# A graph network on one core: three layernorm chunks placed behind the listed rows, shorter update stages, and units of 58 blocks

## What is computed

```python
src, dst = edge_index                      # 25000 edges, dst sorted
denom = jnp.maximum(segment_sum(ones, dst, 50000), 1.0)
conv = lambda x, W, b: segment_sum(concatenate([x[src], edge_attr], axis=1) @ W + b, dst, 50000) / denom[:, None]
outputs = [conv(x, W0, b0)]                # x is 50000 x 128
for W, b in ((W1, b1), (W2, b2), (W3, b3)):
    outputs.append(conv(concatenate(outputs, axis=1), W, b))
result = layernorm(x + outputs[-1])        # over 128 columns, eps 1e-5
```

## Time and profile before

| | us |
|---|---|
| median of three runs | 1026.16 (1024.44 to 1027.6) |
| the profiled execution, its own time | 1026.18 |
| its span, first to last instruction | 1024.2 |
| POOL busy | 719.3 (70%) |
| DVE busy | 698.9 (68%) |
| ACT busy | 497.8 (49%) |
| PE busy | 462.8 (45%) |

### The profile page before, as it was taken

The page is one execution under the profiler, slowest core; times in us unless marked ns, Lnnn a source line. Parts: engine busy times, 40 slices in busy tenths (PEclk is TensorE's granted clock), DMA queues, the critical chain, the costliest instruction groups (busy, mean ns, idle before and its releaser), DMA issues.

```text
span 1024.2 us, 13421 instructions
## 1 busy us (share of the span) xinstructions
PE 462.8 (45%) x2853; PEld 343.8 (34%) x2876; DVE 698.9 (68%) x2449; ACT 497.8 (49%) x1322; POOL 719.3 (70%) x660
## 2 busy tenths in 40 slices
PE   3343663776765899988726300550046661000000
PEld 2342553554443566654415200440035451000000
DVE  6995888788766787667477586659479963798000
ACT  6552765666563667566532155624474640366200
POOL 6674777677771777777767387748777774777775
PEclk9565665656665899999966555675557766555555
DMA  6799569499999476755567389957999982653110
GB/s 181 235 289 271 148 151 295 118 330 318 318 311 339 167 242 230 235 200 190 197 199 248 121 205 298 344 184 191 300 301 349 316 275 56 198 165 134 52 51 32
DMA packets 224614, 224.90 MB, mean 220 GB/s; under 512 B 19218, under 2 KB 206475, under 8 KB 224495
## 3 DMA queue, kind: packets, MB, share of 16 engines
q1 hardware_dynamic: 193551, 153.22, 48.3%
q0 software_dynamic: 26624, 44.81, 16.3%
q10 hardware_dynamic: 4320, 25.56, 6.2%
HBM read 117.11 MB, written 132.74 MB: 244 GB/s over the span
## 4 chain that ended last, share of the span: by engine, by line
DVE 24%; POOL 20%; DMA 16%; issue 12%; PE 11%; ACT 6%; SPq 6%; DVEq 2%; ACTq 1%; POOLq 0%
POOL G L674 6%; POOL out_rows L713 5%; SPq L491 4%; POOL part_rows L687 4%; POOL x_and_z_of_nodes L657 4%; DVE area L1040 3%; DMA G<-part_rows,s0r 3%; DMA x_and_z_of_nodes<-area,sum_rows 3%; DMA area<-src_low_rows 3%; ACT area L814 2%; DMA G<-part_rows,previ 2%; DMA area<-x_and_z_of_nodes 2%; PE hp L2071 2%; DVE AC L1605 2%; POOL EC L706 2%
## 5 line engine op out<-in xcount | busy, mean ns | idle before, releaser
L645 POOL DMA_INDIRECT G<-x_in,srci x196 | 214.1, 1092 | 90.4 <-issue 55.4
L657 POOL DMA_INDIRECT x_and_z_of_nodes<-area,sum_rows x144 | 145.6, 1011 | 70.7 <-ACT area L814 39.0
L842 ACT ACTIVATE area<-area,AC 128x128 f32<-128x128 f32 x299 | 117.5, 479 | 44.4 <-DVE AC L1627 44.4
L782 ACT ACTIVATE UT<-segp,UT 128x1 f32 x168 | 44.0, 262 | 126.9 <-PE segp L1830 93.1
L674 POOL DMA_INDIRECT G<-part_rows,s0r x70 | 82.5, 1178 | 24.6 <-issue 17.7
L814 ACT ACTIVATE area<-hp,zero,inv 128x512 f32<-128x512 f32 x72 | 53.3, 778 | 63.2 <-DMA x_and_z_of_nodes<-area,sum_rows 48.0
L706 POOL DMA_INDIRECT EC<-x_and_z_of_nodes,idx x60 | 63.7, 1062 | 28.1 <-issue 16.5
L2065 PE MATMUL segp<-ZERO 128*128 128x390 f16 (+1 forms) x34 | 15.1, 444 | 148.5 <-DVE EC L1647 148.5
L1830 PE MATMUL segp<-SX,G 128*128 128x128 f32 x336 | 79.3, 425 | 3.3 <-ACT SX L768 3.3
L1830 PEld LDWEIGHTS segp<-SX,G 128*128 128x128 f32 x336 | 72.9, 325 | 3.5 <-ACT SX L768 3.5
L713 POOL DMA_INDIRECT out_rows<-UT,idx x60 | 59.1, 986 | 18.3 <-issue 17.7
(11 more groups left out here) (469 smaller groups left out, 1468.7 us busy)
## 6 DMA issues: line engine op xcount, KB each, us to landing
part_rows<-area SPq DMA_DIRECT2D x36, 768.0 KB
area<-x_and_z_of_nodes SPq DMA_DIRECT2D x30, 832.0 KB, 7.2
x_and_z_of_nodes<-ZERO SPq DMA_DIRECT2D x24, 1024.0 KB
x_and_z_of_nodes<-x_in SPq DMA_DIRECT2D x24, 1024.0 KB
area<-x_in SPq DMA_DIRECT2D x23, 832.0 KB, 7.7
out_rows<-area ACTq DMA_DIRECT2D x23, 832.0 KB, 5.4
part_rows<-ZERO SPq DMA_DIRECT2D x14, 768.0 KB, 11.1
area<-src_low_rows SPq DMA_DIRECT2D x28, 224.0 KB
```

Source lines behind the costliest of these rows:

```text
L645: g.indirect_dma_start(G[:, slot, 0:D], None, x, bass.IndirectOffsetOnAxis(ap=srci[:, c:c + 1].bitcast(u32), axis=0), bounds_check=last_no ...
L657: g.indirect_dma_start(XZ2, bass.IndirectOffsetOnAxis(ap=sum_rows[:, c:c + 1], axis=0), HS3[:, b, j, 3 * D:4 * D], None, bounds_check=last ...
L842: last = a.activation(XLS[b][:, k], XLS[b][:, k], ACT.Identity, bias=shift[:, b, r:r + 1], scale=rs[:, b, r:r + 1])
```

## The change

Five edits are made together.

1. `LSTAGE` goes from 7 and 7 to 6 and 6, `LLAST` from 4 to 3, and the last three chunks (`LAFTER = 3`) are done by DVE and ScalarE behind all batches of listed rows. `CHUNK_AT` renumbers: the c-th chunk done is the node range c+3, and the three done last are the ranges 2, 1, 0, that is, nodes 0 to 4991.
2. POOL's puts run in another order. First come blocks 40 to the end of the first unit, after the stores of 27 chunks and the remaining rows (`OPEN_BLOCKS` is 40: a listed block from 40 on has only nodes from 5120 on). Then blocks 26 to 39 behind the store of range 2, blocks 13 to 25 behind that of range 1, blocks 0 to 12 behind that of range 0.
3. The first listed unit is 58 blocks, and batches are counted from each unit's start.
4. The second group of a step is scattered only if the number of destinations needs it (`n_half`, in `counts[12]`); POOL gets one more branch a step, and SyncE waits for the count that is really scattered. With these inputs n_s is 18 and n_half 17.
5. DVE computes `n_half`: one more `tensor_scalar` and one more `loop_steps`.

```diff
-LUNITS = (0, 60, 70, 80, 90, 110, 130, 150, 170, T)
+LUNITS = (0, 58, 60, 66, 76, 90, 110, 140, 170, T)
-LSTAGE = (None, 7, 7)
-LLAST = 4
+LSTAGE = (None, 6, 6)
+LLAST, LAFTER = 3, 3
+LEARLY = LCH - LLAST - LAFTER
+CHUNK_AT = list(range(LAFTER, LCH)) + list(range(LAFTER - 1, -1, -1))
+OPEN_BLOCKS = (LAFTER * LR + LB - 1) // LB * LB
+LBATCH = [[(lo, min(LB, end - lo)) for lo in range(first, end, LB)] for first, end in zip(LUNITS[:-1], LUNITS[1:])]
+LFIRST = [sum(map(len, LBATCH[:u])) for u in range(len(LBATCH) + 1)]
+LSTARTS = {b[0]: LFIRST[u] + i for u, own in enumerate(LBATCH) for i, b in enumerate(own)}
...
             def scatter_step(i):
...
+                scatter_group(2 * i)
+                with e.If(n_half > i):
+                    scatter_group(2 * i + 1)
+                e.sem_inc(s["pool_tick"], 1)
...
-            def last_rows(lo, hi):
-                for b in range(2 * lo, 2 * hi):
-                    if b % LB == 0:
-                        e.wait_ge(s["y_normed"], b // LB + 1)
+            def put_rows(lo, hi):
+                for b in range(lo, hi):
+                    if b in LSTARTS:
+                        e.wait_ge(s["y_normed"], LSTARTS[b] + 1)
...
             for b in range(RING):
-                e.wait_ge(st_o[b], 16 * len(range(b, LCH, RING)))
+                e.wait_ge(st_o[b], 16 * len(range(b, LCH - LAFTER, RING)))
             e.wait_ge(s["rest_out"], 16)
             e.sem_inc(s["pool_tick"], 1)
-            l_units(last_rows)
+            put_rows(OPEN_BLOCKS, LUNITS[1])
+            nested(e, n_l, 1, NU, put_unit)
+            top = OPEN_BLOCKS
+            for c in range(LCH - LAFTER, LCH):
+                e.wait_ge(st_o[c % RING], 16 * (c // RING + 1))
+                put_rows(CHUNK_AT[c] * LR, top)
+                top = CHUNK_AT[c] * LR
...
             l_unit(0)
             nested(e, n_l, 1, NU, l_unit)
+            for c in range(LCH - LAFTER, LCH):
+                sqrt_rows(c)
+                norm_rows(c)
...
             pack_blocks(ES64, epack)
+            link(v.tensor_scalar(cf[:, 4:5], cf[:, 0:1], -float(CG * P), None, ALU.add))
+            loop_steps(cf[:, 4:5], 2 * CG * P, 12, 0)
             loop_steps(cf[:, 0:1], 2 * CG * P, 0, 1)
...
             l_units(last_rows)
+            lnk = Chain(e, s["link_end"])
+            for c in range(LCH - LAFTER, LCH):
+                chunk(c)
+            norm_pending()
```

More of the change, by code:

```diff
@@ L192, in gnn_kernel @@
         cf = sb("cf", [P, 8], f32)
-        counts = sb("counts", [P, 12], i32)
+        counts = sb("counts", [P, 13], i32)
         ut_ = sb("unit_table", [P, 10 * NU], f32)
@@ L568, in _ @@
             e.sem_inc(s["tick_sp"], 1)
-            for b in (0, 1):
-                e.wait_ge(scat[b], n_s * 64)
+            e.wait_ge(scat[0], n_s * 64)
+            e.sem_inc(s["tick_sp"], 1)
+            n_half = e.value_load(counts[0:1, 12:13], min_val=0, max_val=CIT)
+            with e.If(n_half > 0):
+                e.wait_ge(scat[1], n_half * 64)
                 e.sem_inc(s["tick_sp"], 1)
+            e.sem_inc(s["tick_sp"], 1)
             e.wait_ge(s["et_copied"], n_s * 2 + 4)
@@ L650, in _, with scatter_group @@
             e.wait_ge(s["sc_ready"], 1)
-            def scatter_step(i):
[L652 to L658, removed]
+            def scatter_group(q):
+                for j in range(CG):
+                    c = q * CG + j
+                    e.wait_ge(s["p_act"], c + 5)
+                    g.indirect_dma_start(XZ2, bass.IndirectOffsetOnAxis(ap=sum_rows[:, c:c + 1], axis=0), HS3[:, q % 2, j, 3 * D:4 * D], None,
+                                         bounds_check=last_sum, oob_is_err=False).then_inc(scat[q % 2], 16)
+            def scatter_step(i):
+                scatter_group(2 * i)
+                with e.If(n_half > i):
+                    scatter_group(2 * i + 1)
+                e.sem_inc(s["pool_tick"], 1)
+            n_half = e.value_load(counts[0:1, 12:13], min_val=0, max_val=CIT)
             nested(e, n_s, 0, CIT, scatter_step)
@@ L844, in norm_rows @@
                 e.wait_ge(s["act_normed"], c + 1)
-                e.dma_start(ov[c], XLS[b]).then_inc(st_o[b], 16)
+                e.dma_start(ov[CHUNK_AT[c]], XLS[b]).then_inc(st_o[b], 16)
             REST_AT = SBASE[1] + 2
-            for c in range(LCH - LLAST):
+            for c in range(LEARLY):
                 sqrt_rows(c)
@@ L868, in l_unit @@
             def l_unit(u):
-                ts = [(lo // LB, min(LB, T - lo)) for lo in range(LUNITS[u], LUNITS[u + 1], LB)]
-                for i, (t, n) in enumerate(ts):
+                ts = [(LFIRST[u] + i, lo, n) for i, (lo, n) in enumerate(LBATCH[u])]
+                for i, (t, _, n) in enumerate(ts):
                     sqrt_batch(t, n)
@@ L1724, in scale_rows, with stats_batch @@
                         rest_done()
-            def stats_batch(t, n):
+            def stats_batch(t, lo, n):
                 b = t % 2
-                for q in range(t * LB // 2, (t * LB + n) // 2):
+                for q in range(lo // 2, (lo + n) // 2):
                     r = q % WRING
@@ L1749, in stats_batch, with shift_batch @@
                 v.scalar_tensor_tensor(out=var, in0=vs, scalar=1.0 / D, in1=df, op0=ALU.mult, op1=ALU.add).then_inc(s["y_var"], 1)
-            def shift_batch(t, n):
+            def shift_batch(t, _, n):
                 b = t % 2
@@ L1757, in last_rows @@
             def last_rows(lo, hi):
-                ts = [(b // LB, min(LB, T - b)) for b in range(2 * lo, 2 * hi, LB)]
-                for i, (t, n) in enumerate(ts):
-                    stats_batch(t, n)
+                u = LUNITS.index(2 * lo)
+                ts = [(LFIRST[u] + i, at_, n) for i, (at_, n) in enumerate(LBATCH[u])]
+                for i, (t, at_, n) in enumerate(ts):
+                    stats_batch(t, at_, n)
                     if i:
@@ L1763, in last_rows @@
                     if t < LLAST:
-                        chunk(LCH - LLAST + t)
+                        chunk(LEARLY + t)
                 shift_batch(*ts[-1])
```

22 lines of the change are left out of this document (12 added, 10 removed).

## The result

| | before | changed |
|---|---|---|
| median | 1026.88 us (4 executions, 1024.44 to 1028.21) | 1044.49 us (4 executions, 1040.11 to 1047.7) |
| ratio to before, 95% interval | | 1.0171 [1.0124, 1.0219] |
| span of the profiled execution | 1024.2 | 1038.2 (its own time: 1040.11) |
| last final gather ends | 939.50 | 935.07 |
| from there to the first put | 0.30 | 20.80 |

The change makes the kernel 1.7% slower. The time lies 11 us above the end of the range on record. Everything ahead of the puts became 4.4 us shorter in this execution, and the tail 18.4 us longer.

The account below looks back on a forecast made before the run. The prediction took POOL's queue to bound the kernel's gather and put stages. First put +3.95, two puts fewer -2.6 and stretched puts +2.2 gave +3.55 us, so 1029.7 us, range 1025.0 to 1033.5.

Parts of the forecast that it names:

- my sum: Whole span of 1024.2 us: first put +3.95, two puts fewer -2.6, stretched puts +2.2, together +3.55.
- The first put waits for batch 4: Ahead of the puts: first put 10.65 us behind the last gather's start, POOL idle about 9.5 us.
- The adds under the puts: During the puts: two of the moved chunks' three DVE adds stretch a POOL put by 1.1 us each, +2.2.
- The late stores come in time: During the puts: first moved chunk's store lands at 962, asked for at 968, slack 6 us; all three cost 0.
- The updates: Updates 1 and 2: one chunk fewer each shortens stretched gathers by 0.2 and 0.9 us; the rest is hidden behind POOL.
- rival A: Updates: their chunks are on the path, each removed one gives back 5.3 us; 1020.2 us, chance 0.13.
- Edit 3: Final gathers and puts: 58 blocks save two gathers, -2.75 us, and two puts, -2.6 us.
- Edits 4 and 5: Scatters before round 1: skipping four gives -0.9 us; the count, hidden under waits near 100 us, and the branches cost 0.
- C: POOL waits more: at block 39 for the first late store (+3), or for branches among the scatters (+5.4); chance 0.10.
- B: Later put paid back: skipped scatters bring over 0.9 us, or stretches under puts are missing; 1025.4 to 1028, chance 0.25.

Follow-up runs that it names:

- e1_rest_early: The changed kernel with the store of the last 80 rows issued five chunks earlier in SyncE's program: 1036.56 us, ratio 1.0089 to before.
- e4_rest_again: The same kernel as e1_rest_early, run again on another chip: 1033.78 us, ratio 1.0066 to before.
- e0_again: The changed kernel without an edit, run again on another chip: 1043.31 us, ratio 1.0162 to before.
- e3_half_only: e2_no_after with the first unit back at 60 blocks, leaving only the skipped scatters, their branch and the count: 1029.0 us, ratio 1.0014 to before.
- e2_no_after: The changed kernel with no chunk moved and puts from block 0 on; 58 blocks and skipped scatters stay: 1024.56 us, ratio 0.9981 to before.
- e8_order_only: e5_units_only with blocks 40 to 57 put first, then 0 to 39: 1030.16 us, ratio 1.0055 to before.
- e7_high_first: e1_rest_early with blocks 40 to 57 also gathered and normalized first: 1028.75 us, ratio 1.0012 to before.
- e9_high_fast: e7_high_first without the count and the skip, each moved chunk's shift taken ahead of the next chunk's statistics: 1023.45 us, ratio 0.9984 to before.
- e5_units_only: e2_no_after without the count and the skip, leaving only the first unit of 58 blocks: 1023.69 us, ratio 0.9969 to before.
- e10_units_again: e5_units_only repeated on the chip of e8_order_only and e9_high_fast: 1023.6 us, ratio 0.9979 to before.
- e6_count_only: The kernel before plus DVE's count of half steps, which nobody uses: 1028.79 us, ratio 1.0005 to before.

## Why the prediction was wrong, step by step

**The step that failed** is in the paragraph on edit 2 and the one on the stores: "Now it needs batch 4", and "Do the stores come in time? ... Cost 0". I listed three late stores and one late batch, and left out that the first put waits for `rest_out` too, whose place in SyncE's queue is behind the z load that the moved statistics now hold. The wait and its queue could both be read before: the earlier trace rows name SyncE's queue in the chain, the order printed for POOL shows `rest_out` among the waits of the first put, and the trace of before has the store at 900.25, right behind the last z load. I followed POOL's, DVE's and ScalarE's queues past the moved work, and not SyncE's. Its price is 9.0 and 9.3 us in the two pairs of profiles (e1_rest_early, e4_rest_again), mean 9.1. With the 9.0 of the first pair my sum gives 1027.75 + 9.0 = 1036.8 for the span. The rest of the 1038.2 is 0.4 more in the tail and 1.0 at the last gather's end.

**What the whole executions add.** The median, 1044.49, lies 4.4 us above the profiled execution, and e1_rest_early and e4_rest_again have 1034.9 where I forecast 1029.7. So a second part of the miss, 4 to 5 us, should lie outside the tail. My sum made everything ahead of the tail 5.4 us shorter. By medians e0_again is 16.4 us above the kernel before on its chip, with a tail 18.5 longer, so ahead of the tail it won about 2 (an estimate, since tails are seen in profiles alone). The likeliest place of the missing 3 us is edits 4 and 5: e3_half_only, which has only them, stands 2.1 us above before by medians with the tail of before, where I had -0.9. But e2_no_after stands only 0.9 above the kernels without them, so this second cause stays open.

**The first put waits for batch 4** (+10.15 + 0.5 behind the last gather's start, a gap of 9.5 us): right. The gap is 9.80 and 9.78 once SyncE's wait is gone. The order of the puts alone brings 8.6 us of gap in e8_order_only, and the gap disappears when the order of the gathers follows (e7_high_first).

**The adds under the puts** (+2.2, two adds of 1.1): right in sum where SyncE's wait is gone (2.5 in e1_rest_early), by luck in part; in the changed kernel itself one put is stretched, by 0.7. There are three stretched puts and not two, since DVE's first add starts 2.6 to 2.9 us behind the end of the units and meets the first put. Their excess over 0.98 (1.02 for the first put) is 0.57, 1.33 and 0.57 in e1_rest_early; over the four kernels whose puts start early the 12 values have a mean of 1.02 and go from 0.51 to 1.58. What sets the size can be read from the ends. These are DVE's first two adds in e1_rest_early:

```profile
942.41 1.89 DVE L1650 TENSOR_TENSOR LATE<-LATE,area 128x1664 f32<-128x1664 f32 x1 [2.62 <-issue]
...
947.68 1.88 DVE L1650 TENSOR_TENSOR area<-area 128x1664 f32<-128x1664 f32 x1
```

They end at 944.30 and 949.56, and the stretched puts printed above at 945.20 and 950.42, 0.90 and 0.86 us later. In all 12 cases the stretched put ends 0.85 to 0.91 us behind the add's end, wherever in the add it began, while the put already under way when the add begins keeps its 0.98 (946.82 there). So a put that begins under an add is held until the add ends, and pays what is left of the add. By the page "SBUF — State Buffer" of the Trainium skill, section "SBUF: two separate sides", whichever of the two engines starts first has the shared ports for its whole instruction and blocks the other, if the VectorE instruction has two inputs in SBUF, as this add has, and the GpSimd one reads SBUF (the put has its index tile there). The trace agrees: most of the 1.89 us is paid by a put that begins early in the add (1.58, 1.56), little by one that begins late (0.51). The page's sentence on descriptors that cannot be written, which the prediction gives without a condition, is about VectorE's two-port modes.

**The late stores come in time**: right where the puts start late (no wait in e1_rest_early). In e7_high_first the puts start 9.5 us earlier behind the last gather, the slack of 6 us is used up, and POOL waits 2.65 us for the first store.

**The updates** (-0.2 and -0.9): too small to be seen, and rival A falls. From POOL's start of update 2 to the end of round 3, six kernels with six chunks there (the changed one, e0, e1, e4, e7, e9) need 152.7 to 156.6, mean 154.5, and seven with seven chunks 153.9 to 156.9, mean 154.8. From update 1 to the end of round 2 the means are 93.9 and 93.3. A chunk fully on the path would have shown 5.3 us in each of the two stretches. e9_high_fast says the same of the whole kernel.

**Edit 3** (-2.75 and -2.6): of two gathers and two puts, -5.3, e2_no_after, e5_units_only and e10_units_again give back some 2 us in the wait for the last chunk's store. I had looked for what the first put waits for only in the order of the batches. The medians have -2.2 to -2.9 against before, and e2_no_after stands 4.4 below e3_half_only. The direction was right, and with four chunks among the batches the sum is too large by that wait. The changed kernel, with three, does not have it.

**Edits 4 and 5** (-0.9 and 0): mis-sized, with the wrong sign. The skip brought 0 as far as the profiles show, since the last count comes 5.1 to 5.3 us ahead of round 1 whatever the scatters do; my bound of 0 was the value. The count was not covered by the waits near 100 us: DVE's wait for the low rows, which ended at 98.67 before, ends at 98.7 to 99.4 in the five profiles without the count and at 99.8 to 100.4 in the eight with it (99.95 in the changed kernel, 99.96 in e6_count_only), so the awaited transfers themselves come later, by 0.9 on average. By the profiles the two together cost 1 to 2 us; by medians e2_no_after against e5_units_only and e10_units_again has 0.9, which the spread of the executions could make alone. Its sign is thus likely and its size open.

**The rivals.** C had the right sign and the wrong places: no wait at block 39, no branch costs in the scatter stage. B's first half (a large gain by skipped scatters) is refuted by e3_half_only, its second (no stretch) by e1_rest_early.

**What stays open.** The profiled executions of the changed kernel, e0_again, e1_rest_early and e4_rest_again lie 1.6 to 6.8 us under their own medians, those of the others on either side. The tails of two profiles agree, so the spread should lie ahead of the puts; no run here shows where.

## What to carry to other kernels

When an instruction group is moved behind others, go through every in-order queue that waits for its signal, the one that only issues transfers first of all, and list what stands behind that wait and who needs it. An instruction that waits for many signals hides all but the latest; when the work ahead of it gets shorter, as with 58 blocks, the next one shows. A transfer whose data are ready early belongs in the queue ahead of loads that wait for late work. And before work is taken off an engine, look whether the queue that sets the pace shows gaps that this engine ends: here there were none, so moving chunks had nothing to win.

## What the runs showed of the hardware

A gather or put of POOL that begins while DVE's add of a chunk (128x1664, two inputs, 1.89 us) runs is held until the add ends. The 12 stretched puts end 0.85 to 0.91 us behind the add; in round 3 of the kernel before, the nine stretched gathers end 0.86 to 0.95 us behind it. The price is what is left of the add, from 0.51 to 1.58 us for a put and up to 1.90 for the gather of the earlier trace rows at 755.63. Where the two begin within 0.2 us of each other, either may go first.

A gap that the profile calls "issue" can be a wait for a transfer: the 2.25 to 2.35 us ahead of the first put in the kernels with 58 blocks and four chunks among the batches (e2, e5, e10) end 0.8 us behind the landing of the last chunk's store, where the landing is on record (e2, e10). With 60 blocks (before, e3, e6) this store lands ahead of the put's turn, and in e7 and e9 no such late store is there.

DVE has an "issue" gap of 2.6 to 2.9 us between the last `shift_batch` and the first moved chunk, behind the branch over the units that are not needed. In all six kernels with moved chunks a transfer of the queue that the profile names "instruction" falls into it, in the changed kernel within 940.9 to 943.8:

```profile
q14 instruction: 1, 0.01, 0.7%
```

So it is likely the time in which the code behind the branch is loaded. No run tried it.
